# Gathers that may lead TensorE by 16 tiles instead of 8, scatters 34 gathers behind instead of 27

## The reference

```python
logits = -dist2 + jnp.einsum('bld,ed->ble', x, rw) + rb
topv, topi = jax.lax.top_k(logits, TOP_K)               # 4 of 16 experts
w = jax.nn.softmax(topv, axis=-1)
hidden = jax.nn.gelu(jnp.einsum('bld,efd->blef', x, w1) + b1, approximate=False)
exp_out = jnp.einsum('blef,edf->bled', hidden, w2) + b2
sel = jnp.take_along_axis(exp_out, topi[..., None], axis=2)
fused = jnp.sum(w[..., None] * sel, axis=2)
```

## Time and profile before

| | |
|---|---|
| time, median of 3 runs | 700.9 us (699.55 to 707.57) |
| span of the profiled execution | 694.4 us |
| around the span, to the median | 6.5 us |
| expert loop in it | first gather at 229.6 us, last scatter at 664.6 us |
| TensorE matmuls busy | 536.4 us, 77% of the span |
| GpSimd busy | 281.1 us, of it 125.5 in 128 gathers, 128.3 in 128 scatters |

### The profile page before, as it was taken

One profiled execution on the slowest core, in us unless ns is written; L12 is line 12 of the kernel. 1 busy time (PEld: TensorE's weight loads), 2 busy tenths in 40 slices (PEclk: granted clock), 3 DMA queues, 4 the chain that ended last, 5 costly groups with the idle time before them and its releaser, 6 DMA issues.

```text
span 694.4 us, 19926 instructions
## 1 busy us (share of the span) xinstructions
PE 536.4 (77%) x6242; PEld 481.6 (69%) x6242; DVE 364.9 (53%) x1325; ACT 353.7 (51%) x1079; POOL 281.1 (40%) x308
## 2 busy tenths in 40 slices
PE   4999879994502789977678789789977776679984
PEld 4967779993401489976677679678967776668942
DVE  6554779997999356545434553112334432233126
ACT  6524167775556365546445667336634434335513
POOL 4000000000451543566666743664566666645520
PEclk9999999998655799999999999999999989989998
DMA  8970000006001455444444645445866644546553
GB/s 229 255 280 9 3 3 0 0 0 243 1 1 76 120 161 157 138 131 131 131 140 143 204 124 162 135 144 146 264 207 180 183 130 133 145 122 192 174 197 122
DMA packets 55746, 92.28 MB, mean 133 GB/s; under 512 B 10352, under 2 KB 26096, under 8 KB 55152
## 3 DMA queue, kind: packets, MB, share of 16 engines
q1 hardware_dynamic: 45424, 72.35, 35.0%
q0 software_dynamic: 10240, 18.89, 9.2%
HBM read 78.07 MB, written 17.37 MB: 137 GB/s over the span
## 4 chain that ended last, share of the span: by engine, by line
PE 43%; issue 18%; DVE 18%; POOL 8%; ACT 7%; DMA 2%; DVEq 2%; another core or an unknown queue 0%; POOLq 0%; SPq 0%; ACTq 0%
PE bank L2148 15%; PE bank L2141 13%; POOL yd L600 6%; ACT value L883 3%; DVE shared L1187 2%; DVE shared L1179 2%; POOL shared L592 2%; DVE early L1467 2%; PE bank L1735 2%; DMA shared<-yd 1%; PE bank L1772 1%; PE bank L1840 1%; PE bank L1762 1%; PE bank L2133 1%; PE bank L2089 1%
## 5 line engine op out<-in xcount | busy, mean ns | idle before, releaser
L883 ACT ACTIVATE value<-bank,shared 128x128 f32<-128x128 f32 x632 | 180.8, 376 | 203.0 <-PE bank L2141 156.7
L2148 PE MATMUL bank<-shared,value 128*128 x1264 | 182.7, 290 | 62.4 <-ACT value L883 41.7
L2148 PEld LDWEIGHTS bank<-shared,value 128*128 128x128 f32 x1264 | 161.7, 200 | 76.7 <-issue 76.1
L2141 PE MATMUL bank<-early,shared 128*128 x1264 | 180.9, 288 | 5.3 <-issue 2.8
L592 POOL DMA_INDIRECT shared<-xd,early x128 | 125.5, 980 | 127.5 <-PE bank L2141 79.8
L2141 PEld LDWEIGHTS bank<-early,shared 128*128 128x128 f32 x1264 | 162.6, 200 | 9.3 <-issue 8.4
L1663 DVE SCALAR_TENSOR_TENSOR early<-bank,value,early 128x128 f32 x158 | 55.4, 351 | 195.8 <-PE bank L2148 116.6
L600 POOL DMA_INDIRECT yd<-early x128 | 128.3, 1002 | 67.8 <-DVE early L1663 36.2
L560 POOL TENSOR_TENSOR shared<-shared,xn 128x512 f32<-128x512 f32 x4 | 5.1, 1264 | 174.9 <-DVE xn L1262 167.1
L2133 PE MATMUL bank<-ident,shared 128*128 128x128 f32 x128 | 35.9, 284 | 9.0 <-DMA shared<-xd,early 5.7
L2003 PE MATMUL bank<-ksp,shared 128*128 128x32 bf16 x1536 | 40.9, 177 | 0.0
(11 more groups left out here) (334 smaller groups left out, 689.3 us busy)
## 6 DMA issues: line engine op xcount, KB each, us to landing
shared<-w1b SPq DMA_DIRECT2D x158, 258.0 KB
w1b<-in_w_t SPq DMA_DIRECT2D x1, 4096.0 KB, 17.8
shared<-col_dram SPq DMA_DIRECT2D x1, 4096.0 KB, 13.4
shared<-in_w_t SPq DMA_DIRECT2D x1, 4096.0 KB, 12.3
att<-yd SPq DMA_DIRECT2D x8, 512.0 KB
shared<-yd SPq DMA_DIRECT2D x4, 1024.0 KB, 9.1
xd<-xnT SPq DMA_DIRECT2D x2, 1280.0 KB
shared<-xd,early POOLq DMA_INDIRECT x128
```

Source lines behind the costliest of these rows:

```text
L883: ins = act.activation(hT[:, i % 2, tok(c)], bank[2 + i % 2][:, tok(c)], ACT.Gelu, bias=w1_now[:, i % WR, F + c:F + c + 1])
L2141: ins = mm(bank[2 + i % 2][:, tok(c)], w1_now[:, i % WR, tok(c)], x_now, start=True, stop=True)
L2148: ins = mm(bank[6 + i % 2][:, 0:D], hT[:, i % 2, tok(c)], w2_sb[:, bass.ds(e, 1), c, :] .rearrange("p a d -> p (a d)"), start=(c == 0), st ...
```

## The change

`NEAR` becomes 16 and `BEHIND` 34. Both are used in GpSimd's queue alone.

```diff
@@ -48,10 +48,10 @@
     RING = 8
     SLOTS = 32
     LEAD = 3
-    BEHIND = 27
+    BEHIND = 34
     GRP = 4
     XR = 24
-    NEAR = 8
+    NEAR = 16
     XSEM = 12
```

## The result

The changed kernel took 712.3 us, median of 4 runs (710.5 to 714.4), against 703.2 us for the kernel before on the same chip (699.6 to 707.6): ratio 1.0138, 95% interval 1.0091 to 1.0186. By the ratio that is 9.7 us slower; differences in us are worked out from ratios in this way throughout, so they can lie some tenths of a us beside the difference of the medians. The likeliest case was 706.0 us. The profiled execution's span is 711.6 us at a mean clock of 0.899; before it was 694.4 at 0.923.

What follows compares the result with a forecast made beforehand. Unbroken runs of GpSimd issues were taken to hold TensorE's signals until about 1 us after their end. Terms 10.0 - 7.8 + 12 - 8.5 - 1.5 + 1 = +5.2 on 700.9 gave 706 us, range 687 to 714.

Steps and rivals of the forecast that it cites:

- 1. The start: Start of the loop: 8 more gather issues in the first run delay TensorE's signals, +10.0 us, bounds 0 and +11.
- 2. The first part's alternation: First part, gathers and scatters alternating: seven steps at 3.03 us become 1.91, -7.8 us, bounds -5 and -10.
- 3. The middle: Where the second part's gathers begin among scatters 51 to 63: longer issue runs hold signals, +12 us, bounds -4 and +15.
- Who waits for the scatters?: Scatters throughout the loop: standing one step nearer to the result they need was costed at 0.
- hangs on the sorting, not on a lead: Middle: the first wait for a gather's landing, 2.77 us, was to stay despite the longer lead.
- Rival c): Alternation: scatters wait for their y_add, 0.3 us per pair of steps, +9 on the forecast, 715 us; chance 0.09.
- 4. The second part: Second part: seven alternating steps fewer, -8.5 us, and the run behind the last gather one issue shorter, -1.5 us.
- 5. The clock: TensorE's granted clock: two longer stalls more and a few short ones less, +1 us, bounds 0 and +3.
- The anchor: Whole kernel: the profiled execution of 694.4 us with 6.5 us around it makes the median of 700.9.
- a) no hold: Long issue runs: signals pass, the start costs 2 and the middle nothing, 685 us; chance 0.19.
- b) half held: Long issue runs: signals leak now and then, centre 697 us; chance 0.17.
- d): Gathers: the ring of 24 and 12 gathers in flight hold them back, so nothing changes, 701 us; chance 0.05.

Runs made afterwards that it cites:

- start_burst: Kernel before, but gathers 0 to 15 wait for no up; later gathers lead by 8, scatters 27 behind: 709.0 against 698.2 us, ratio 1.0147.
- start_paused: Changed kernel with one memset that nobody reads ahead of each of gathers 8 to 15: ratio 1.0063 to the kernel before.
- scatter_dropped: Kernel before without its 128 scatters, GpSimd only raising the semaphore that each landing would raise: ratio 0.886 to the kernel before.
- behind_34: Kernel before with scatters 34 behind and the lead still 8: ratio 1.0125 to the kernel before.
- ramp_first_part: Changed kernel, lead growing from 8 every third gather in the first part; second part at lead 8, scatters 27 behind: ratio 0.9878 to the kernel before.
- ramp_early: Changed kernel, but the lead grows from 8 to 16 before the scatters begin, in both parts: 688.3 against 698.5 us for the kernel before, ratio 0.9875.

## Why the prediction was right or wrong

The time fell inside the range, 6 us above the forecast, and on the slower side of the 1% bound, where I had given 0.29 against 0.46 for no change. The mechanism was the right one. Sizes were off, all to one side, by 10 us together in the trace, so that the range held is owed in part to its width of 27 us. By the trace, in the prediction's steps:

*1. The start, +10.0.* Measured 13.1 - 2.0 = 11.1 us, just over the upper bound of 11. gelu(1) at 253.8, the run of 17 gathers to 251.5: as said. start_burst shows that this is the burst's own cost, and the rows of start_paused that signals pass where there are pauses.

*2. The first part's alternation, -7.8.* Measured 13.1 to 8.5, -4.6. The step that failed is 7 x 1.12: the saved steps are those with side work, and scatter_dropped puts them at 2.22 us without a second issue. 7 x 0.8 = 5.6, and behind_34, which changes nothing else up to there, gains 5.8 from up(8) to up(48). The bound of -5 had that reason in it; I took the wrong end.

*3. The middle, +12.* Measured 8.5 to 24.0, +15.5, just past the bound of +15. The first run was to have 7 issues more, 11 in all against 4 before (431.77 to 436.6), and to cost 9 us. It had 9 and cost 6.3: the difference is +8.5 at up(72) and +14.8 at up(73). "Who waits for the scatters? ... 0" is what was wrong there, since scatter 55 waited for its y_add. Afterwards it did go on "at GpSimd's pace": +15.6 at up(82). TensorE was at up(81) when scatter 63 had gone, as said. What failed is the run after that. Gathers 77 to 81 came in one row as told, but scatters 61 to 63 and gathers 75 and 76 stood right ahead of them without a pause. That made 10 issues and not 5; TensorE did one step in them, up(82), and not two, and up(83) came at +24.1, 8.5 us for this run alone. Wrong too was that the wait of 2.77 us for the first landing "hangs on the sorting, not on a lead": it hung on up(71). With the longer lead gather 64 started 0.3 us behind the sorting and some 4 us ahead of up(72), and none of the four waits for a landing is left in the loop. Rival c) as told, steps over 3.1 us in the alternation, did not occur (3.01 and 3.03).

*4. The second part, -8.5 and -1.5.* Measured 24.0 to 17.2, -6.8. From up(128) on 10.4 us are won back, just over the "8 to 10 us" that I named; but 3.6 us were lost before that in the alternation, from up(88) to up(128), which no step of mine has. The run at the turn got shorter by 7.82 - 5.17 = 2.7 us of gelu's idle time.

*5. The clock, +1.* It is inside the figures above. The granted clock fell to 0.82 in the middle, and TensorE's matmuls were busy for 539.5 - 536.4 = 3.1 us more. That is all that the rows say of its price; no run isolates it.

*The anchor.* "6.5 us around it" was wrong: the profiled execution of the changed kernel took 713.4 us for a span of 711.6, so 1.8 us lie around a span, and the rest of the 6.5 was that the profiled run of before was a short one. Its medians in the later comparisons were 698.2 to 701.3 us. The sum of the steps in the loop is 15.2 and not 5.2; the timed difference is 9.7 (6.4 to 13.1). Which of the two single executions is to blame for the distance isn't settled.

*The rivals.* a) no hold: fell with start_burst. b) half held: its 697 fell, but its leaks exist, as gelu(6) in start_paused and the gelu at 404.89 in behind_34 show, both of which start before their run ends. c) is in part in step 3. d) fell: gather 16 is issued at 251.5 instead of 257.3. The Trainium skill, "Trainium Architecture — The Big Picture", section "What this means for kernel authors", has engines block each other only through a semaphore; these traces disagree: in start_burst gelu(1) starts 9.8 us after the end of its up (248.75 to 258.51), with GpSimd's issues between them, and neither engine waits for GpSimd there.

**What the forecast had missed as a whole.** There are 256 transfers and 158 steps. A step carries one at no cost that I saw and a second for 0.8 to 1.14 us. A longer lead takes no transfer away: it puts eight gathers earlier and takes seven pairs out of the alternation. It gains only if the eight fall where there is slack, which is what ramp_first_part and ramp_early did, and it loses if they fall in one run, as in the change. Had I seen this sum as a conservation, the start and the alternation would have been set against each other, and I would have looked for slack and not for a lead.

## What to carry to other kernels

When an engine issues many small transfers, count issues against the steps of the loop: a change of lead or order moves issues and removes none, so ask into which steps they move and whether those have slack. Don't let permissions come in a burst. A lead that grows by one every few steps, ahead of the stretch in which a second kind of transfer joins, gave 1.2% here, where the same lead at once cost 1.4%. And read the waits of the engine that is waited for after a change, not only in the alternation but right behind each long stall.

## What the runs showed that I had not expected

- A pause of 0.8 us between issues of a run was enough to let TensorE's signals through in the end, but the first one came 4.4 us late; plain GpSimd work between two gathers held none in the stretch shown.
- The first gather is issued at 229 to 231 us in some executions and at 235.3 to 235.5 in others, in kernels that are the same up to there. So 5 to 6 us of difference between two single traces can lie ahead of the loop. The loop itself repeats well: from up(8) to up(157) start_burst, which has before's code there, ended 1.0 us apart, though the difference between them moved by 4.8 us on the way.
- What holds the signals is not shown by any run. Shown is when it happens, and not to the last one: up(0)'s signal passed inside the first run, up(1)'s in the same run did not, and what tells them apart stays open.
